# Zero rows for the unused token slots: scattered by number instead of filled over all slots

## The chip, the cores and the metric

The kernel runs on one core of a Trainium2 chip. The metric is the device time of one execution in microseconds. Before the change it is 575.49 us, the median of 3 runs (574.5 to 575.81).

## What is computed

The input `x` is 4 sequences of 512 tokens with 256 numbers each (2048 tokens). It is normalised, and the result `xn` goes two ways. One is a gated linear attention block with an MLP (`s`); the other a mixture of experts (`g`). The output joins them:

```python
xn = _layernorm(x)
# attention: q, k, v, g and a decay per head, then for each time step
S = S * jnp.exp(gt)[..., None] + kt[..., None] * vt[..., None, :]
ot = jnp.einsum('bhk,bhkd->bhd', qt, S)
# then head norm, silu gate, Wo, rmsnorm, MLP
# experts: 16 of them, the best 4 for each token, weights normalised over the 4
act = jax.nn.silu(g) * u
out = jnp.einsum('bske,keh->bskh', act, down_proj)
sel = jnp.take_along_axis(out, top_idx[..., None], axis=2)
return jnp.sum(sel * top_w[..., None], axis=2)
# whole: x + s * silu(experts)
```

## The kernel before

All waits between engines are written out by hand as semaphores; each engine runs its own list in order.

**Routing and slots.** Every (token, expert) pair gets a slot. The slots of one expert fill whole tiles of 128, so 80 tiles (10240 slots, `SLOTS`) are set aside for 8192 pairs; 2048 slots stay without a token. A slot is a row of `rows_scratch` in device memory with 274 numbers (`ROW`): the normalised token, its scale, its token number and its expert weights. A row without a token must hold zeros and a token number beyond the real ones, since the expert stage multiplies it and adds the result to the row of that number in `y_scratch`.

**The zero fills.** `zrow` on the chip is such an empty row for each of 128 partitions (written by POOL, L487 and L488). ScalarE (ACT) issues 16 DMAs (`zero`, L636, called at L700) of 640 rows each, two in each step `u` of the first batch's attention, each behind one activation that normalises `xn` (L698). They cover all 10240 rows and count up `zero_fill`. Eight more fills of `y_scratch` (`y_zero`) come later.

**Order in the first batches.** The attention of a batch takes 8 steps `u`. In a step, VectorE (DVE) does `kv` (L951) and two scans `st` (L959); GpSimd (POOL) multiplies them by q (`product`, L529); TensorE sums them up (`read_out`, L1247). The k and decay of a batch lie in PSUM banks, which ACT fills for the next batch in `next_banks` (L677), when the last `kv` and the last scan of the batch are done. DVE computes the routing (L985 to L1037) as a chain of instructions that wait for each other; between them it puts pieces of the recurrence of steps 6 and 7 of batch 0 and 0 and 1 of batch 1. At its end it counts up `route_ready`; `name_tiles` (L1042 to L1047) then says which expert owns a tile.

**The scatters.** POOL writes the rows to their slots with 64 indirect DMAs of 128 rows (`scatter`, L558). From batch 1's step 0 on it issues two in each step, behind the step's `product`. Ahead of the first pair it waits for `route_ready` and `zero_fill`. The loop `turns` runs on when the products are over, so the last 16 scatters follow one another at once. SyncE (SP) waits for all of them before it loads 16 tiles of rows into `X` (L452), and behind those it issues the two loads of the down weights `wd` (L448), of 14 and of 2 experts. TensorE waits for both `wd` loads after the first tile's gate and up products, ahead of its loop over the tiles.

**The expert stage.** For each of 80 tiles TensorE transposes X (L1276), does 6 gate and up products (L315), transposes the hidden rows (L1374) and does 4 down products; ACT and DVE do what lies between, and POOL adds the result to `y_scratch` (L586). At the end DVE, ACT and POOL combine it with `xn` and `x`.

The line that counts for the entry into this stage:

```python
sp.wait_ge(s["tpn_ready"], KC * B)
sp.wait_ge(s["scatter"], 16 * NT * TOP)
for u in range(UN):
    load_rows(0, u)
load_down(0, E - 2)
sp.wait_ge(s["gu_ready"], 2 * NF * B)
load_down(E - 2, E)
...
gate_up(0, 0, e_first)
pe.wait_ge(s["wd_in"], 32)
tiles(0, True, False)
```

Of the kernel before, what the change touches and what calls it, by code (L numbers as in the profile page):

```python
# [5 lines left out]
F32 = mybir.dt.float32  # L6
# [3 lines left out]
U32 = mybir.dt.uint32  # L10
ALU = mybir.AluOpType
# [3 lines left out]
P = 128  # L15
# [24 lines left out]
def build_block(nc, x, Wq, Wk, Wkg1, Wkg2, bkg2, Wv, Wg, bg, Wo, ln1_w, ln2_w, W1, W3, W2,  # L40
# [3 lines left out]
    T = B * L  # L44
# [14 lines left out]
    SLOT_TILES = -(-(T * TOP // P + E - 1) // 4) * 4  # L59
    SLOTS = SLOT_TILES * P  # L60
    ROW = D + 2 + E
    SCALE_C, TOKEN_C, WEIGHT_C = D, D + 1, D + 2
# [23 lines left out]
    with ExitStack() as ctx:  # L86
# [3 lines left out]
        def sb(name, shape, dt, scope=ctx):  # L90
            return scope.enter_context(nc.sbuf_tensor(name, shape, dt))


        xn = sb("xn", [P, NT, D], F32)
        ident = sb("ident", [P, P], F32)
        ident16 = sb("ident16", [P, P], F16)
# [9 lines left out]
        restart = sb("restart", [P, NT, E], F32)  # L106
        one_e = sb("one_e", [P, E], F32)
        steps128 = sb("steps128", [P, E, NT], F32)
        tile_no = sb("tile_no", [1, SLOT_TILES], F32)
# [29 lines left out]

        zrow_f = sb("zrow", [P, 2 * P + 32], F32, att)  # L140
        zrow = zrow_f[:, 0:ROW]
        sb("fill1", [P, KC * 2 * I - 2 * P - 32], F32, att)

# [18 lines left out]
        def rsb(name, shape=(P, NT, E), dt=F32):  # L162
            return sb(name, list(shape), dt, rt)
# [20 lines left out]
        prod = rsb("prod")  # L184
        slot_f = rsb("slot_f", (P, TOP, NT))
        rt.close()
        pre.close()
# [57 lines left out]
            an_ready anhi_ready anlo_ready xn_ready wk1_t wk1_copied wz_ready rw_t wprep_act wprep_dve w13_in  # L245
            wo_in w2_in zero_fill tp_ready proj_ready evac_act evac_dve z_ready zs_ready
            a_ready dve_chain pool_chain act_chain exp_ready m16_ready cum_ready route_ready ex_in
            scatter zero_row bz_neg wv_mean wv_ready dve_max vt_ready vt_out0 vt_out1 prep_done vr_in0 vr_in1
# [70 lines left out]

        U = HD // 2  # L320
        TOK = lambda b: bass.ds(b * L, L)
        TILES = lambda b, i=0, n=TPB: bass.ds(b * TPB + i, n)
# [53 lines left out]
        def _(sp):  # L376
# [58 lines left out]
            sp.wait_ge(s["gla_used"], U * B + 2)  # L435
            sp.wait_ge(s["zero_fill"], 16 * NT)
            sp.wait_ge(s["y_zero"], 16 * U)
# [16 lines left out]
            sp.wait_ge(s["tpn_ready"], KC * B)  # L454
            sp.wait_ge(s["scatter"], 16 * NT * TOP)
            for u in range(UN):
# [27 lines left out]
        def _(pool):  # L484
# [7 lines left out]
            for m in (ident, ident16):  # L492
# [11 lines left out]
            step(nc.gpsimd.iota(steps128[:, :, :], pattern=[[0, E], [P, NT]], base=0, channel_multiplier=0,  # L504
                                allow_small_or_imprecise_dtypes=True))
            nc.gpsimd.iota(tile_no[:, :], pattern=[[1, SLOT_TILES]], base=0, channel_multiplier=0,
                           allow_small_or_imprecise_dtypes=True).then_inc(s["const_pool"], 1)
# [45 lines left out]

            scatters = iter([(t, j) for t in range(NT) for j in range(TOP)])

            def scatter(n):
                for _, (t, j) in zip(range(n), scatters):
                    nc.gpsimd.indirect_dma_start(  # L558
                        rows_dram, bass.IndirectOffsetOnAxis(ap=slot_u[:, j, t:t + 1], axis=0),
                        rows[:, t, :], None).then_inc(s["scatter"], 16)  # L560

            def step_fn(a, b, c, u):
                if a is not None:
                    if u == 0:
                        pool.wait_ge(s["evac_act"], len(ACT_NTH) * a + ACT_NTH[Q_OUT])
                    product(a, u)
                if b == 0 and u == 0:
                    pool.wait_ge(s["route_ready"], 1)
                    pool.wait_ge(s["zero_fill"], 16 * NT)
                if b is not None:  # L570
                    scatter(2)

            turns(pool, step_fn)
            pool.wait_ge(s["pool_turn"], U * B)
            pool.wait_ge(s["scatter"], 16 * NT * TOP)

# [26 lines left out]
        def _(act):  # L603
# [87 lines left out]
            for u in range(U):  # L691
# [4 lines left out]
                for t in (2 * u, 2 * u + 1):  # L696
                    act.wait_ge(s["an_ready"], t + 1)
                    nc.scalar.activation(xn[:, t, :], xn[:, t, :], ACT.Identity, scale=rsq[:, 0, t:t + 1],  # L698
                                         bias=shift[:, 0, t:t + 1]).then_inc(s["xn_ready"], 1)
                    zero(rows_dram[t * (SLOTS // NT):(t + 1) * (SLOTS // NT)], "zero_fill")  # L700
                if u == 4:
# [144 lines left out]
        def _(dve):  # L846
# [177 lines left out]
            step(nc.vector.tensor_tensor(base[:, :], ntc[:, :], ntl[:, :], ALU.subtract))  # L1024
            step(nc.vector.tensor_scalar(base[:, :], base[:, :], float(P), None, ALU.mult))
            step(nc.vector.tensor_tensor(inc[:, :, :], inc[:, :, :], tot[:, :, :], ALU.subtract))
            step(nc.vector.tensor_tensor(slot[:, :, :], CUM, inc[:, :, :].rearrange("p e t -> p t e"), ALU.add))
# [4 lines left out]
            for j in range(TOP):  # L1032
# [3 lines left out]
                step(nc.vector.tensor_reduce(slot_f[:, j, :], prod[:, :, :], AX.X, ALU.add))  # L1036
            nc.vector.tensor_copy(slot_u[:, :, :], slot_f[:, :, :]).then_inc(s["route_ready"], 1)  # L1037

            def name_tiles():
# [392 lines left out]
```

## Time and profile before

| | us |
|---|---|
| median of 3 runs | 575.49 (574.5 to 575.81) |
| the profiled execution | 574.92 |
| its span, first to last instruction | 572.9 |
| PE busy | 429.3 (75%) |
| DVE busy | 345.0 (60%) |
| POOL busy | 304.7 (53%) |
| ACT busy | 230.9 (40%) |
| DMA, mean share of the 16 engines | q1 (SP) 31.6%, q0 (POOL) 20.0%, q10 (ACT) 8.5% |

PE is TensorE's matmuls. The share of busy time is a mean over stages with different limits: up to about 345 us the engines take turns in the attention, from there on the expert stage runs. L followed by a number is a line of the kernel. In a timeline a row says when an instruction started, how long it took, on which engine and line, and in brackets how long the engine had been idle before it and for what; a "q" behind an engine's name is its queue of orders, DMA issues among them. "issue" stands for time in which the engine waited for nothing that the profile shows. Time from issue to landing is that of a DMA.

### The profile page before, as it was taken

The page shows a single profiled execution, that of the slowest core. Times are in us where ns is not written, and L with a number is a line of the kernel's source. Part 1 is how long each engine was busy: PE and PEld are TensorE (multiplying, and loading weights), DVE is VectorE, ACT ScalarE, POOL GpSimd, SP SyncE. Part 2 cuts the span into 40 slices and gives each one's busy share as a digit, 9 for nine tenths or more (in the row PEclk, how much of TensorE's full clock was granted, in tenths as well). Part 3 has the DMA queues.
Part 4 walks back from the last instruction along what each step waited for, and adds up shares of the span by engine and source line. Part 5 has one row for each costly group of instructions (what it writes and reads, how often), then busy time and mean ns, then how long its engine had stood idle before and what let it go on. Part 6 is the DMA issues. An engine that isn't in the chain of part 4 may idle for free.

```text
span 572.9 us, 8861 instructions
## 1 busy us (share of the span) xinstructions
PE 429.3 (75%) x2170; PEld 254.9 (44%) x2171; DVE 345.0 (60%) x613; ACT 230.9 (40%) x521; POOL 304.7 (53%) x230
## 2 busy tenths in 40 slices
PE   2479970313568798699889989999999999999400
PEld 1134320101223354255465557767767767677200
DVE  4665867999989979985755633333333333333065
ACT  0526642300133132122554525556655656566221
POOL 4052695146768468576720006656566656666535
PEclk9989996655759899899999999999999999999855
DMA  8334998745535234232988845666666666664493
GB/s 265 110 111 160 304 330 279 270 150 171 186 123 185 89 126 151 106 114 65 357 288 238 176 149 85 112 101 114 103 112 112 112 102 110 111 85 57 55 318 121
DMA packets 78616, 90.42 MB, mean 158 GB/s; under 512 B 7704, under 2 KB 66808, under 8 KB 78584
## 3 DMA queue, kind: packets, MB, share of 16 engines
q1 hardware_dynamic: 47584, 54.82, 31.6%
q0 software_dynamic: 14592, 19.47, 20.0%
q10 hardware_dynamic: 16408, 15.73, 8.5%
q8 instruction: 16, 0.26, 0.2%
q14 instruction: 16, 0.13, 0.1%
HBM read 50.66 MB, written 39.34 MB: 157 GB/s over the span
## 4 chain that ended last, share of the span: by engine, by line
PE 54%; DVE 19%; issue 9%; DMA 8%; POOL 4%; ACT 2%; ACTq 2%; SPq 0%; POOLq 0%; DVEq 0%
PE mm_ps L315 33%; PE sum_ps L315 12%; DVE st L959 4%; PE turn_ps L1276 3%; DVE kv L951 3%; PE mm_ps L1374 3%; POOL qs L529 2%; DMA rows_scratch<-zrow 2%; DMA eb<-n_L_ffn_expert_bias_dram 2%; PE sum_ps L1247 2%; DVE w_gu L1181 2%; DMA vrep<-v_scratch 1%; DMA y_scratch<-y,X 1%; ACTq L636 1%; DVE ghead L1111 1%
## 5 line engine op out<-in xcount | busy, mean ns | idle before, releaser
L586 POOL DMA_INDIRECT y_scratch<-y,X x80 | 124.3, 1554 | 126.7 <-ACT y L815 96.6
L315 PE MATMUL mm_ps<-w_gu,xT 128*128 x480 | 103.9, 352 | 1.6 <-DVEq L1159 1.5
L529 POOL TENSOR_TENSOR qs<-st,q_sb 128x1024 f32<-128x1024 f32 x32 | 75.4, 2356 | 49.0 <-DVE st L959 24.3
L1071 DVE TENSOR_TENSOR xT<-turn_ps,xT 128x256 f16<-128x256 f32 x80 | 33.9, 425 | 88.0 <-ACT xT L726 88.0
L315 PE MATMUL sum_ps<-wd,hT 112*128 x320 | 82.4, 380 | 0.0
L558 POOL DMA_INDIRECT rows_scratch<-rows,slot_u x64 | 64.0, 1001 | 27.2 <-issue 15.1
L959 DVE TENSOR_TENSOR_SCAN st<-sum_ps,kv 128x512 f32<-128x512 f32 x64 | 75.1, 1210 | 1.0
L315 PE MATMUL mm_ps<-an2T,w 128*128 128x512 f16 x264 | 65.1, 403 | 13.6 <-DVE h_mlp L1080 11.1
L1247 PE MATMUL sum_ps<-qs,sumk 128*32 128x512 f32 x128 | 38.2, 710 | 38.5 <-POOL qs L529 37.2
L315 PEld LDWEIGHTS mm_ps<-w_gu,xT 128*128 128x128 f16 x480 | 46.6, 97 | 33.0 <-issue 2.7
L1164 DVE SCALAR_TENSOR_TENSOR h<-mm_ps,X,sl 128x224 f32<-128x224 f32 x80 | 36.1, 451 | 40.9 <-ACT sl L799 40.9
L315 PEld LDWEIGHTS sum_ps<-wd,hT 112*128 112x128 f32 x320 | 54.3, 190 | 4.7 <-issue 0.2
L815 ACT ACTIVATE y<-sum_ps,X 128x256 f32<-128x256 f32 x80 | 38.0, 474 | 44.3 <-PE sum_ps L315 44.3
L799 ACT ACTIVATE sl<-mm_ps,X 128x224 f32<-128x224 f32 x80 | 35.8, 447 | 43.4 <-PE mm_ps L315 43.4
L315 PE MATMUL mm_ps<-anT,w_a 128*128 128x512 f16 x168 | 43.0, 414 | 11.2 <-DVE anT L912 9.2
L315 PEld LDWEIGHTS mm_ps<-an2T,w 128*128 128x128 f16 x264 | 26.3, 103 | 54.1 <-issue 16.6
L315 PE MATMUL mm_ps<-w,h_mlp 128*128 128x256 f32 x192 | 47.8, 394 | 1.0 <-DVE h_mlp L1080 1.0
L951 DVE TENSOR_TENSOR kv<-vrep,mm_ps 128x1024 f32<-128x1024 f32 x32 | 38.8, 1212 | 5.6 <-ACT mm_ps L677 4.1
L315 PEld LDWEIGHTS mm_ps<-w,h_mlp 128*128 128x128 f32 x192 | 33.9, 189 | 14.5 <-issue 10.0
L732 ACT ACTIVATE sg<-mm_ps 128x512 f32<-128x512 f32 (+1 forms) x24 | 14.3, 597 | 46.8 <-PE mm_ps L315 46.8
L1276 PE MATMUL turn_ps<-ident,X 128*128 128x128 f32 x160 | 30.7, 274 | 2.5 <-issue 2.5
L315 PEld LDWEIGHTS mm_ps<-anT,w_a 128*128 128x128 f16 x168 | 16.9, 105 | 34.9 <-issue 17.8
(165 smaller groups left out, 533.4 us busy)
## 6 DMA issues: line engine op xcount, KB each, us to landing
vrep<-v_scratch SPq DMA_DIRECT2D x64, 256.0 KB
rows_scratch<-zrow ACTq DMA_DIRECT2D x16, 685.0 KB, 11.7
X<-rows_scratch SPq DMA_DIRECT2D x80, 137.0 KB, 2.6
w_gu<-y_scratch SPq DMA_DIRECT2D x16, 256.0 KB, 6.1
y_scratch<-zrow ACTq DMA_DIRECT2D x6, 640.0 KB, 5.9
w_gu<-in_L_ffn_gate_proj_dram SPq DMA_DIRECT2D x16, 224.0 KB, 6.8
w_gu<-in_L_ffn_up_proj_dram SPq DMA_DIRECT2D x16, 224.0 KB, 7.1
wd<-in_L_ffn_down_proj_dram SPq DMA_DIRECT2D x1, 3136.0 KB, 17.4
```

What stands on the lines that cost most here:

```text
L315: last = nc.tensor.matmul(out_ap, lhsT, rhs, start=(n == 0), stop=(n == len(pairs) - 1))
L529: nc.gpsimd.tensor_tensor(qs[:, u % 2, :, :], st[:, u % 2, :, :], pair_bc(q_sb[:, TOK(a)]), ALU.mult).then_inc(s["qs_ready"], 1)
L558: nc.gpsimd.indirect_dma_start(rows_dram, bass.IndirectOffsetOnAxis(ap=slot_u[:, j, t:t + 1], axis=0), rows[:, t, :], None).then_inc(s["sc ...
L586: nc.gpsimd.indirect_dma_start(y_dram[u % 2], bass.IndirectOffsetOnAxis(ap=X[:, u, TOKEN_C:TOKEN_C + 1].bitcast(U32), axis=0), y[:, u, :], ...
L799: nc.scalar.activation(sl[:, u % 2, :], M[u % 2][:, 0:I], ACT.Silu, scale=X[:, u, SCALE_C:SCALE_C + 1])\
L815: nc.scalar.activation(y[:, u, :], sum_ps[:, u % 2, 0:D], ACT.Copy, scale=X[:, u, bass.ds(e + WEIGHT_C, 1)])\
L951: nc.vector.tensor_tensor(kv[:, r, :, :], vrep[:, r, :, :], pair_bc(K_BANK), ALU.mult).then_inc(s["kv_ready"], 1)
L959: nc.vector.tensor_tensor_scan(st[:, r, j, :], A_BANK, kv[:, r, j, :], 0.0, ALU.mult, ALU.add).then_inc(s["st_ready"], 1)
L1071: nc.vector.tensor_tensor(xT[:, u % 2, 1, :, :].rearrange("p c n -> p (c n)"), PS[u % 2][:, 0:KC * P], xT[:, u % 2, 0, :, :].rearrange("p ...
L1164: nc.vector.scalar_tensor_tensor(out=h[:, u % 2, :], in0=M[u % 2][:, I:2 * I], scalar=X[:, u, SCALE_C:SCALE_C + 1], in1=sl[:, u % 2, :], o ...
L1247: last = nc.tensor.matmul(O0[rows_at:rows_at + QUARTER, :], sumk[:, off:off + QUARTER], qs[:, u % 2, j, :], start=(dd % PER == 0), stop=(d ...
L1276: last = nc.tensor.transpose(PS[u % 2][:, n * P:(n + 1) * P], X[:, u, n * P:(n + 1) * P], ident[:, :])
```

## The change

ACT's 16 zero fills and the semaphore `zero_fill` go. The numbers of the 2048 slots without a token are computed by DVE: four instructions on 128x16 join the routing chain, and five (three of them on 128x256) follow behind `route_ready` and count up `pads_ready`. POOL writes the empty rows to them with 16 indirect DMAs of 128 rows. The row scatters start at step 2 of batch 1 rather than at step 0, and the four that this displaces are done in the last round of `turns`, in which there are no products; the 16 scatters of empty rows stand there too, four in each of the first four steps. SP and POOL wait for 80 scatters in place of 64.

```diff
+    PADS = SLOTS - T * TOP
+    NPAD = PADS // P
...
+        zrow = sb("zrow", [P, ROW], F32)
...
+        pad_no = sb("pad_no", [P, NPAD], F32)
+        pad_u = sb("pad_u", [P, NPAD], U32)
...
+        held, pads_to, past, pad_f = mx, need, eqc[:, 0:NPAD, :], sm[:, 0:NPAD]
...
+        SCATTER_FROM = 2
...
-            sp.wait_ge(s["zero_fill"], 16 * NT)
...
-            sp.wait_ge(s["scatter"], 16 * NT * TOP)
+            sp.wait_ge(s["scatter"], 16 * (NT * TOP + NPAD))
...
+            step(nc.gpsimd.iota(pad_no[:, :], pattern=[[P, NPAD]], base=0, channel_multiplier=1,
+                                allow_small_or_imprecise_dtypes=True))
...
+            def scatter_pads(n):
+                for _, i in zip(range(n), pads):
+                    nc.gpsimd.indirect_dma_start(
+                        rows_dram, bass.IndirectOffsetOnAxis(ap=pad_u[:, i:i + 1], axis=0),
+                        zrow[:, :], None).then_inc(s["scatter"], 16)
...
-                if b == 0 and u == 0:
+                if b == 0 and u == SCATTER_FROM:
                     pool.wait_ge(s["route_ready"], 1)
-                    pool.wait_ge(s["zero_fill"], 16 * NT)
-                if b is not None:
+                if b == 1 and u == 0:
+                    pool.wait_ge(s["pads_ready"], 1)
+                if b is not None and (b > 0 or u >= SCATTER_FROM):
                     scatter(2)
+                if b == B - 1 and u < U // 2:
+                    scatter(2)
+                    scatter_pads(-(-NPAD // (U // 2)))
...
-                    zero(rows_dram[t * (SLOTS // NT):(t + 1) * (SLOTS // NT)], "zero_fill")
...
+            step(nc.vector.tensor_tensor_scan(held[:, :], one_e[:, :], inc[:, :, NT - 1:NT].rearrange("p e a -> p (e a)"), 0.0,
+                                              ALU.mult, ALU.add))
+            step(nc.vector.tensor_tensor(pads_to[:, :], base[:, :], held[:, :], ALU.subtract))
+            step(nc.vector.tensor_copy(held[:, :], inc[:, :, NT - 1:NT].rearrange("p e a -> p (e a)")))
+            step(nc.vector.tensor_tensor(pads_to[:, :], pads_to[:, :], held[:, :], ALU.add))
...
             nc.vector.tensor_copy(slot_u[:, :, :], slot_f[:, :, :]).then_inc(s["route_ready"], 1)
+
+            of_e = lambda ap: ap.rearrange("p (a e) -> p a e", a=1).to_broadcast((P, NPAD, E))
+            step(nc.vector.tensor_tensor(past, of_e(pads_to[:, :]),
+                                         pad_no[:, :].rearrange("p (i a) -> p i a", a=1).to_broadcast((P, NPAD, E)), ALU.is_le))
+            step(nc.vector.tensor_tensor(past, past, of_e(held[:, :]), ALU.mult))
+            step(nc.vector.tensor_reduce(pad_f, past, AX.X, ALU.add))
+            step(nc.vector.tensor_tensor(pad_f, pad_f, pad_no[:, :], ALU.add))
+            nc.vector.tensor_copy(pad_u[:, :], pad_f).then_inc(s["pads_ready"], 1)
```

## Rows read from the trace of the kernel before

**Rows 1.** Busy time by stretch (us, PE, PEld, DVE, ACT, POOL, clock, DMA share, GB/s)

```profile
345.00:525.00 180.00, 178.20 (x1017) 127.18 (x1016) 63.26 (x145) 107.05 (x290) 112.81 (x73) 1.00 0.64 103
315.00:320.00 5.00, 5.00 (x25) 2.29 (x24) 3.38 (x4) 2.83 (x5) 0.00 (x0) 1.00 1.13 256
189.00:193.00 4.00, 3.89 (x11) 1.48 (x12) 3.96 (x6) 0.60 (x1) 0.00 (x0) 0.58 0.09 35
```

**Rows 2.** The chain of waits, 80 to 135 us (start us, us, what)

```profile
97.99 12.98 DMA rows_scratch<-zrow
...
111.01 10.68 issue
```

**Rows 3.** Timeline of ACT near 100 us (start, us, engine, line, what [idle before])

```profile
100.43 0.60 ACT L677 ACTIVATE mm_ps<-k_sb 128x512 f32<-128x512 f32 x1 [1.86 <-issue]
```

**Rows 4.** Timeline of DVE, 90 to 127 us

```profile
93.31 2.27 DVE L1000 TENSOR_TENSOR_SCAN eqc<-restart,eq 128x256 f32<-128x256 f32 x1
...
101.16 1.22 DVE L951 TENSOR_TENSOR kv<-vrep,mm_ps 128x1024 f32<-128x1024 f32 x1 [4.15 <-ACT mm_ps L677]
102.30 0.42 DVE L1003 TENSOR_TENSOR eq<-eq,eqc 128x256 f32<-128x256 f32 x1
...
111.42 0.69 DVE L1017 TENSOR_TENSOR_SCAN inc<-restart,tot 128x256 f32<-128x256 f32 x1
...
113.28 0.17 DVE L1024 TENSOR_TENSOR base<-ntc,ntl 128x16 f32<-128x16 f32 x1
...
125.03 1.86 DVE L1047 TENSOR_SCALAR tile_expert<-own 1x80 uint32<-1x80 f32 x1
126.81 1.20 DVE L951 TENSOR_TENSOR kv<-vrep,mm_ps 128x1024 f32<-128x1024 f32 x1
```

**Rows 5.** Timeline of POOL, 92 to 127 us

```profile
92.19 2.85 POOL L539 TENSOR_TENSOR w<-w_raw,w 128x1408 f16<-128x1408 f32 x1
96.86 2.35 POOL L529 TENSOR_TENSOR qs<-st,q_sb 128x1024 f32<-128x1024 f32 x1 [1.83 <-DVE st L959]
108.29 2.36 POOL L529 TENSOR_TENSOR qs<-st,q_sb 128x1024 f32<-128x1024 f32 x1 [9.08 <-PE sum_ps L1247]
...
124.47 2.35 POOL L529 TENSOR_TENSOR qs<-st,q_sb 128x1024 f32<-128x1024 f32 x1
```

**Rows 6.** Timeline of POOL, 263 to 290 us

```profile
263.99 2.35 POOL L529 TENSOR_TENSOR qs<-st,q_sb 128x1024 f32<-128x1024 f32 x1 [3.54 <-DVE st L959]
...
279.18 0.96 POOL L558 DMA_INDIRECT rows_scratch<-rows,slot_u  x1 [0.30 <-issue]
...
288.97 1.23 POOL L558 DMA_INDIRECT rows_scratch<-rows,slot_u  x1 [0.30 <-issue]
```

**Rows 7.** All instructions on `rows_scratch`, their DMAs

```profile
DMA to landing us min/median/max: 2.0/2.8/13.3
```

**Rows 8.** Timeline of the SP queue, 300 to 322 us

```profile
300.45 7.46 SPq L452 DMA_DIRECT2D X<-rows_scratch  x16
307.95 13.82 SPq L448 DMA_DIRECT2D wd<-in_L_ffn_down_proj_dram  x2
```

**Rows 9.** DMA issues between 300 and 340 us (x, KB each, us to landing)

```profile
wd<-in_L_ffn_down_proj_dram SPq DMA_DIRECT2D x1, 3136.0 KB, 17.4
X<-rows_scratch SPq DMA_DIRECT2D x16, 137.0 KB, 3.3
...
wd<-in_L_ffn_down_proj_dram SPq DMA_DIRECT2D x1, 448.0 KB, 7.4
```

**Rows 10.** Timeline of PE, around 189 us and 336 us

```profile
176.95 2.76 PE L315 MATMUL mm_ps<-an2T,w 128*128 128x512 f16 x12
...
189.11 4.34 PE L315 MATMUL mm_ps<-an2T,w 128*128 128x512 f16 x12 [4.73 <-DVE h_mlp L1080]
...
321.26 0.60 PE L1276 MATMUL turn_ps<-ident,X 128*128 128x128 f32 x4
...
336.36 1.31 PE L315 MATMUL mm_ps<-w_gu,xT 128*128 x6 [1.53 <-DVEq L1159]
```

More of the change, by code:

```diff
@@ L60, in build_block @@
     SLOTS = SLOT_TILES * P
+    PADS = SLOTS - T * TOP
+    NPAD = PADS // P
+    assert PADS % P == 0
     ROW = D + 2 + E
@@ L138, in build_block @@
         qs = sb("qs", [P, 2, 2, L], F32, att)
-        zrow_f = sb("zrow", [P, 2 * P + 32], F32, att)
-        zrow = zrow_f[:, 0:ROW]
-        sb("fill1", [P, KC * 2 * I - 2 * P - 32], F32, att)
+        sb("fill1", [P, KC * 2 * I], F32, att)
         g_sb = sb("g_sb", [P, KC, T], F32, att)
@@ L245, in build_block @@
             an_ready anhi_ready anlo_ready xn_ready wk1_t wk1_copied wz_ready rw_t wprep_act wprep_dve w13_in
-            wo_in w2_in zero_fill tp_ready proj_ready evac_act evac_dve z_ready zs_ready
-            a_ready dve_chain pool_chain act_chain exp_ready m16_ready cum_ready route_ready ex_in
+            wo_in w2_in tp_ready proj_ready evac_act evac_dve z_ready zs_ready
+            a_ready dve_chain pool_chain act_chain exp_ready m16_ready cum_ready route_ready pads_ready ex_in
             scatter zero_row bz_neg wv_mean wv_ready dve_max vt_ready vt_out0 vt_out1 prep_done vr_in0 vr_in1
@@ L554, in _ @@
             scatters = iter([(t, j) for t in range(NT) for j in range(TOP)])
+            pads = iter(range(NPAD))
             def scatter(n):
@@ L566, in step_fn @@
                     product(a, u)
-                if b == 0 and u == 0:
+                if b == 0 and u == SCATTER_FROM:
                     pool.wait_ge(s["route_ready"], 1)
-                    pool.wait_ge(s["zero_fill"], 16 * NT)
-                if b is not None:
+                if b == 1 and u == 0:
+                    pool.wait_ge(s["pads_ready"], 1)
+                if b is not None and (b > 0 or u >= SCATTER_FROM):
                     scatter(2)
+                if b == B - 1 and u < U // 2:
+                    scatter(2)
+                    scatter_pads(-(-NPAD // (U // 2)))
             turns(pool, step_fn)
             pool.wait_ge(s["pool_turn"], U * B)
-            pool.wait_ge(s["scatter"], 16 * NT * TOP)
+            pool.wait_ge(s["scatter"], 16 * (NT * TOP + NPAD))
             pool.sem_inc(s["y_slots"], UN)
```

## The prediction

> **What bounds the kernel now.** I read the busy time by stretch first. From 345 to 525 us TensorE is busy for 178.2 of 180 us at the full granted clock [rows 1]: the expert stage is TensorE's alone, so whatever the change does before it reaches the end undiminished, and nothing after it can absorb a delay. The change touches two earlier places, the routing (80 to 127 us) and the entry into the expert stage (265 to 340 us).
>
> The chain of waits names the last zero fill, 12.98 us from its issue to its landing at 110.97, and then 10.68 us of "issue" [rows 2]. That is not the price of the fill: POOL's wait for it ends at 110.97, but the slot numbers it also waits for exist only at 121.69. What the fills do cost is ScalarE's time. Its queue issues them, and the bank fills of batch 1 (L677) stand behind the last of them; the first starts at 100.43, with "issue" as the reason for the idle time [rows 3]. VectorE waits for that bank: 4.15 us idle before the `kv` product at 101.16 [rows 4], in the middle of its otherwise unbroken routing work. That wait is the gain to be had.
>
> **Part 1: the zero fills go.** With ScalarE free, the K bank is filled as soon as `kv_ready` allows, before 97.0, when VectorE is free (101.16 less 4.15). The A bank needs the last scan of batch 0, done just before POOL's product at 96.86 [rows 5], plus a 0.60 copy [rows 3]: 97.5, wanted at 98.2, when `kv` is done. So the whole 4.15 goes. -4.15.
>
> **What is late next.** POOL's products then meet VectorE elsewhere. The rows show the effect: the 128x256 scan L1000 takes 2.27 us while POOL works from 92.19 to 95.04, the scan of the same shape L1017 takes 0.69 with POOL idle, and L1047, on 80 numbers, takes 1.86 beside the product at 124.47 [rows 4, 5]. The Trainium skill, "SBUF — State Buffer", section "Who interferes with whom", says that a VectorE instruction with two SBUF inputs contends with a GpSimd instruction that reads SBUF, the later one waiting for the whole of the other; the rows just named agree, and without the rule the front part would come out at about -3.1.
> - L1003 moves from 102.30 to 98.15, inside POOL's product of 96.86 to 99.21. It ends some 0.25 after that instead of at 98.57: +0.9.
> - `product(1, 1)` no longer waits behind `route_ready`. Before, it runs at 124.47. Its state and read-outs are ready when `product(1, 0)` ends, so it follows at once: 105.0 to 107.4 for the first (108.29 less 3.25), to 109.75 for the second. L1017 would start at 108.2; by L1000, which ends 0.54 after POOL, it ends at 110.3 and not at 108.9: +1.4.
> - The other side: L1047 no longer has a product beside it. At about 0.25 us for its 80 numbers: -1.6.
>
> **Part 2: the numbers of the pads, on VectorE.** Four instructions on 128x16 stand ahead of `route_ready`; such a one takes 0.17 (L1024) [rows 4], with the gap of a chained step some 0.21: +0.85. After it come three on 128x256 at 0.42 (as L1003) and two small ones, 1.8 us with gaps. POOL scatters nothing yet, so these don't hold it, but `name_tiles` and the next `kv` (126.81) stand behind them on VectorE: +1.8.
> Front sum: -4.15 + 0.9 + 1.4 + 0.85 + 1.8 - 1.6 = **-0.8**. Bounds: -3.1 with no collision; +0.2 if POOL keeps VectorE out over both products; I take the sum that reads each collision from its nearest row. The iota for `pad_no` and the larger constants stand at the start, under the wait for the first loads: 0.
>
> From there to 266 us POOL does two scatters beside each product, as before; only the first four move. The 4 extra row scatters thus fall to the end, where VectorE and TensorE set the pace, and all carry the -0.8.
>
> **Part 3: 20 more scatters behind the last product.** Before, 18 scatters follow the product of 263.99 and the last starts at 288.97. After, 4 more of rows and 16 of pads follow. Each takes 0.96 and 0.30 of idle time, 1.26 [rows 6]; a pad's has the same shape. 20 x 1.26 = 25.2, so the last starts at 288.97 + 25.2 - 0.8 = 313.4, and with the 2.8 us median to landing [rows 7] it is there at 316.2.
>
> Who waits: SyncE's queue has `scatter` ahead of the 16 loads of X, and both `wd` loads stand behind those. Before, SyncE goes on at 300.45, on TensorE's word; the scatters were no matter. It spends 7.46 us on the X loads and issues the large `wd` load at 307.95 [rows 8], which lands 17.4 later; the small one takes 7.4, much of it behind the large one [rows 9]. After: X from 316.2. The first X tile lands by 319.5 with the 3.3 of [rows 9]; TensorE turns it at 321.26 [rows 10] less 0.8: hidden, by 1 us only. The large `wd` is issued at 316.2 + 7.5 = 323.7 and lands at 341.1; the small one directly behind it, by bytes 17.4 x 448/3136 = 2.5, at 343.6.
>
> TensorE waits for both before its tile loop, right after its first six expert products (336.36 + 1.31 = 337.67 [rows 10], less 0.8 = 336.9). Stall: 343.6 - 336.9 = **6.7**. Bounds: 3.4 (the small load rides along, landing 2.0) to 12 (21 us for both, as from 307.95 to the last landing before, and 6.8 us of queueing for the scatters).
>
> **Part 4: the clock after the stall.** After 4.73 us of idle time twelve products take 4.34 instead of 2.76 [rows 10], at a granted clock of 0.58 of full speed in that stretch, the lower level of 1.2 GHz for most of it [rows 1]. A stall of 6.7 should do the same: **+1.6** (bounds 0 and 4).
>
> **Sum.** -0.8 + 6.7 + 1.6 = +7.5. The profiled execution took 574.92 (span 572.9); 582.4 for it, and against the median of 575.49, which is 0.57 above it: **583.0**.
>
> **The rivals.**
> - *The weights are in time (faster).* TensorE waits only if `wd` is in later than 336.9, so 3.67 MB within 13.2 us of 323.7, 278 GB/s. For it: the large load alone ran at 185 GB/s while it shared the engines with the last X loads, and TensorE would need only 6.7 us. Against it: from 315 to 320, with nothing but `wd` moving, the 16 engines were full (share 1.13) at 256 GB/s [rows 1]. Then the front decides: 575.49 - 0.8 to - 3.1, 572.4 to 574.7. Chance 0.17. The Trainium skill, "DMA: Bandwidth & Descriptors", section "Measured (HBM→SBUF, 128 partitions, SWDGE, issued from GpSimd)", has 1 MB at 341 GB/s; an estimate from that page is 11 us for both loads and no stall, but the 17.4 measured here for the same transfer decides.
> - *Between:* the scatters land sooner and the small load costs nothing; a stall near 3.4, little loss of clock, front at -3.1 to -0.8: 576.5 to 580. Chance 0.13.
> - *No gain in front:* the bank comes late for another reason (POOL's last product, a load of `vrep`), and only the added work is left: +3.35 instead of -0.8, with the same stall behind it: 587. Chance 0.12. For it: VectorE never waited on anything else there, so nothing shows what is next. Against: each producer is done by 97.5.
> - *Main case,* 580 to 586.5: 0.58.
>
> **How the numbers follow.** The forecast is the main case's, 583.0. A range of 576.5 to 588 takes in the two slower cases and the between one; what is left out is mostly the rival of in-time weights. This kernel's measurement tells 0.2% (1.15 us) from no change: faster 0.16, same 0.06, slower 0.78.
>
> **What would show it.** Right: no ScalarE DMA issue of `rows_scratch`; the 4.15 us before L951 gone; the L1017 scan near 2 us; 38 scatters behind the last product, ending near 315; SyncE's wait for `scatter` some 16 us longer; the `wd` loads issued near 324; TensorE idle for 6 to 7 us at 337 to 344. Wrong: no gap on TensorE there; POOL done before 305; or the first `kv` of batch 1 still late.

## The result, and the profile after

| | before | after |
|---|---|---|
| median | 575.65 us, 4 runs (574.5 to 575.97) | 586.32 us, 4 runs (584.51 to 587.26) |
| the profiled execution | 574.92 | 587.26 |
| its span | 572.9 | 585.3 |
| DVE busy | 345.0 | 348.7 |
| POOL busy | 304.7 | 321.7 |

The ratio is 1.0185, 95% interval [1.0156, 1.0214]: slower by some 10.7 us. The two profiled executions, which the working compares, differ by 12.34 us.

Lines of the kernel after are numbered anew: `kv` L968, `st` L976, `product` L536, the bank fills L695, row scatters L566, scatters of empty rows L572, the matmul helper L320, the turning of X L1306; on SP the loads of X L457 and of `wd` L453.

The queues first: ACT's (q10) carried 15.73 MB and 8.5% of the DMA engines before; after, the same view of the page has

```profile
q1 hardware_dynamic: 47584, 54.82, 32.8%
q0 software_dynamic: 15360, 21.72, 20.7%
q10 hardware_dynamic: 5912, 4.51, 2.5%
```

So the fills are gone and 11.2 MB with them; POOL's queue (q0) carries 2.25 MB more. ACT's timeline in the stretch of [rows 3] has no issue of `rows_scratch` any more, and both banks come early:

```profile
92.28 0.60 ACT L695 ACTIVATE mm_ps<-k_sb 128x512 f32<-128x512 f32 x1 [1.79 <-DVE kv L968]
97.74 0.60 ACT L695 ACTIVATE sum_ps<-a_sb 128x512 f32<-128x512 f32 x1 [4.86 <-DVE st L976]
```

DVE's timeline answers to [rows 4]:

```profile
86.57 1.57 DVE L1012 TENSOR_TENSOR gt<-lg,m 128x256 f32<-128x256 f32 x1
...
97.95 1.21 DVE L968 TENSOR_TENSOR kv<-vrep,mm_ps 128x1024 f32<-128x1024 f32 x1
99.08 1.44 DVE L1020 TENSOR_TENSOR eq<-eq,eqc 128x256 f32<-128x256 f32 x1
...
109.22 2.27 DVE L1034 TENSOR_TENSOR_SCAN inc<-restart,tot 128x256 f32<-128x256 f32 x1
...
113.08 0.19 DVE L1043 TENSOR_TENSOR_SCAN mx<-one_e,inc 128x16 f32<-128x16 f32 x1
...
121.68 0.20 DVE L1059 CAST slot_u<-slot_f 128x64 uint32<-128x64 f32 x1
121.79 0.42 DVE L1062 TENSOR_TENSOR eqc<-need,pad_no 128x256 f32<-128x256 f32 x1
...
126.79 0.19 DVE L1077 TENSOR_SCALAR tile_expert<-own 1x80 uint32<-1x80 f32 x1
126.91 1.20 DVE L968 TENSOR_TENSOR kv<-vrep,mm_ps 128x1024 f32<-128x1024 f32 x1
```

The `kv` at 97.95 has no idle time in front of it where 4.15 us were. But L1020 takes 1.44 instead of 0.42 and the scan L1034 2.27 instead of 0.69, both beside a product of POOL; the naming is fast (0.19 for 1.86). The `kv` behind it starts at 126.91, against 126.81 before: the front has gained nothing.

The price stands at the entry of the expert stage. POOL's timeline first (compare [rows 6]), the last product and then 38 scatters, of which three stand here:

```profile
264.75 2.35 POOL L536 TENSOR_TENSOR qs<-st,q_sb 128x1024 f32<-128x1024 f32 x1 [3.55 <-DVE st L976]
...
274.89 0.96 POOL L572 DMA_INDIRECT rows_scratch<-zrow,pad_u  x1 [0.30 <-issue]
...
286.32 1.86 POOL L572 DMA_INDIRECT rows_scratch<-zrow,pad_u  x1 [0.30 <-issue]
...
316.22 0.96 POOL L566 DMA_INDIRECT rows_scratch<-rows,slot_u  x1 [0.30 <-issue]
```

SP waited 25.2 us for them ahead of the X loads (before, 1.8, and then 5.0 for TensorE). Its queue's timeline, then the DMA issues between 310 and 360 us (x, KB each, us to landing), against [rows 8] and [rows 9]:

```profile
318.89 7.46 SPq L457 DMA_DIRECT2D X<-rows_scratch  x16
326.40 10.49 SPq L453 DMA_DIRECT2D wd<-in_L_ffn_down_proj_dram  x2
336.94 2.28 SPq L467 DMA_DIRECT2D xback<-in_L_attn_x_dram  x1
```

```profile
wd<-in_L_ffn_down_proj_dram SPq DMA_DIRECT2D x1, 3136.0 KB, 18.5
...
xback<-in_L_attn_x_dram SPq DMA_DIRECT2D x1, 2048.0 KB, 17.1
wd<-in_L_ffn_down_proj_dram SPq DMA_DIRECT2D x1, 448.0 KB, 21.7
```

The first `wd` load is issued 18.45 us later than before, and the second lands at 348.6 (issued at 326.9, 21.7 on). TensorE stands still until then, as PE's timeline (against [rows 10]) and the busy time by stretch (columns as in [rows 1]) show:

```profile
337.20 1.31 PE L320 MATMUL mm_ps<-w_gu,xT 128*128 x6 [1.53 <-DVEq L1189]
349.42 0.66 PE L1306 MATMUL turn_ps<-ident,X 128*128 128x128 f32 x2 [10.91 <-DMA wd<-in_L_ffn_down_proj_dram]
349.87 2.45 PE L320 MATMUL mm_ps<-w_gu,xT 128*128 x6
...
354.55 1.03 PE L320 MATMUL sum_ps<-wd,hT 112*128 x4
```

```profile
340.00:345.00 5.00, 0.00 (x0) 0.00 (x0) 0.00 (x0) 0.00 (x0) 0.00 (x0) 0.50 1.13 222
345.00:350.00 5.00, 0.58 (x3) 0.52 (x4) 0.00 (x0) 0.00 (x0) 0.00 (x0) 0.50 1.10 301
350.00:355.00 5.00, 5.00 (x22) 2.97 (x21) 1.30 (x3) 2.04 (x6) 0.00 (x0) 0.66 0.35 109
```

Between 340 and 345 us every compute engine is at zero and the DMA engines are full: only loads are under way, those of the down weights and, behind them, the 2 MB of `xback`. From the turn at 349.42 to the first down product, 5.13 us pass where it took 4.28 before. The same rows of the kernel before:

```profile
337.55 0.41 PE L1276 MATMUL turn_ps<-ident,X 128*128 128x128 f32 x2
...
340.14 0.41 PE L1276 MATMUL turn_ps<-ident,X 128*128 128x128 f32 x2 [0.74 <-issue]
...
341.83 1.03 PE L315 MATMUL sum_ps<-wd,hT 112*128 x4
```

The granted clock was 0.50 from 340 to 350 us (the lower level, 1.2 GHz), and the first six products behind the wait take 2.45 us for 1.31. The restart costs 0.85 us net, because the 0.74 us for which TensorE stood idle at 340.14 in the kernel before are gone.

So the 12.4 us are: entry of the stage (PE's products at 337.20 against 336.36) +0.84, wait +10.91, clock +0.85, sum 12.6. Behind the last matmul 0.5 us come back (36.4 us to the end for 36.9).

### The profile page after: what moved, and what is told of

Read it like the earlier page. It is cut to its first block and busy times, and to the rows that moved or that the text cites. A ratio compares the mean times of both kernels' runs of the same rounds, so it can differ in the third digit from the quotient of the medians.

```text
span 585.3 us, 8870 instructions
## 1 busy us (share of the span) xinstructions
PE 429.6 (73%) x2170; PEld 255.5 (44%) x2171; DVE 348.7 (60%) x622; ACT 231.0 (39%) x521; POOL 321.7 (55%) x247
## 5 line engine op out<-in xcount | busy, mean ns | idle before, releaser
L536 POOL TENSOR_TENSOR qs<-st,q_sb 128x1024 f32<-128x1024 f32 x32 | 75.5, 2362 | 64.6 <-DVE st L976 55.8
L320 PE MATMUL mm_ps<-w_gu,xT 128*128 x480 | 105.2, 356 | 1.6 <-DVEq L1189 1.5
L320 PE MATMUL sum_ps<-wd,hT 112*128 x320 | 82.3, 380 | 0.0
L976 DVE TENSOR_TENSOR_SCAN st<-sum_ps,kv 128x512 f32<-128x512 f32 x64 | 75.0, 1209 | 1.0
L320 PE MATMUL mm_ps<-an2T,w 128*128 128x512 f16 x264 | 64.0, 398 | 15.2 <-DVE h_mlp L1110 12.7
L566 POOL DMA_INDIRECT rows_scratch<-rows,slot_u x64 | 62.8, 981 | 16.3 <-issue 15.4
L320 PEld LDWEIGHTS mm_ps<-w_gu,xT 128*128 128x128 f16 x480 | 47.0, 98 | 33.7 <-issue 3.8
L320 PEld LDWEIGHTS sum_ps<-wd,hT 112*128 112x128 f32 x320 | 54.3, 190 | 4.6 <-issue 0.2
L320 PE MATMUL mm_ps<-anT,w_a 128*128 128x512 f16 x168 | 43.1, 415 | 11.7 <-DVE anT L929 9.6
L320 PEld LDWEIGHTS mm_ps<-an2T,w 128*128 128x128 f16 x264 | 26.0, 102 | 54.8 <-issue 15.0
L320 PE MATMUL mm_ps<-w,h_mlp 128*128 128x256 f32 x192 | 47.8, 394 | 1.0 <-DVE h_mlp L1110 1.0
L1306 PE MATMUL turn_ps<-ident,X 128*128 128x128 f32 x160 | 31.2, 277 | 12.9 <-DMA wd<-in_L_ffn_down_proj_dram 10.9
L320 PEld LDWEIGHTS mm_ps<-w,h_mlp 128*128 128x128 f32 x192 | 33.9, 189 | 14.5 <-issue 10.0
L968 DVE TENSOR_TENSOR kv<-vrep,mm_ps 128x1024 f32<-128x1024 f32 x32 | 38.7, 1210 | 0.7 <-DVE vt L944 0.4
L743 ACT ACTIVATE xT<-turn_ps 128x256 f16<-128x256 f32 x80 | 30.0, 376 | 12.4 <-PE turn_ps L1306 12.3
## 6 DMA issues: line engine op xcount, KB each, us to landing
wd<-in_L_ffn_down_proj_dram SPq DMA_DIRECT2D x1, 3136.0 KB, 18.5
```

The costliest lines, as they stand in the source:

```text
L320: last = nc.tensor.matmul(out_ap, lhsT, rhs, start=(n == 0), stop=(n == len(pairs) - 1))
L536: nc.gpsimd.tensor_tensor(qs[:, u % 2, :, :], st[:, u % 2, :, :], pair_bc(q_sb[:, TOK(a)]), ALU.mult).then_inc(s["qs_ready"], 1)
L566: nc.gpsimd.indirect_dma_start(rows_dram, bass.IndirectOffsetOnAxis(ap=slot_u[:, j, t:t + 1], axis=0), rows[:, t, :], None).then_inc(s["sc ...
L968: nc.vector.tensor_tensor(kv[:, r, :, :], vrep[:, r, :, :], pair_bc(K_BANK), ALU.mult).then_inc(s["kv_ready"], 1)
L976: nc.vector.tensor_tensor_scan(st[:, r, j, :], A_BANK, kv[:, r, j, :], 0.0, ALU.mult, ALU.add).then_inc(s["st_ready"], 1)
L1306: last = nc.tensor.transpose(PS[u % 2][:, n * P:(n + 1) * P], X[:, u, n * P:(n + 1) * P], ident[:, :])
```

## The experiments

Theory: the loss is the wait of TensorE for `wd`, and it comes from the number of scatters behind the last product, by way of SP's queue; the front is a gain and a cost that cancel. Rivals: the added VectorE work or the delayed first scatters cost the time; the load is slow by itself; the fills' removal is worth nothing.

Each is compared with runs of the kernel before on the same chip, whose median there was 573.6 us for `from0`, `x2_first`, `pads_mid` and `late_fills`, 574.09 for `displaced`, `pads_half`, `xback_late` and `combo`, and 584.91, on a third chip, for `before_again`, `late_again` and `numbers`. Four positions are read from each trace: the start of the routing on DVE (`lg`), the `kv` behind the naming, the first products of the expert stage (the "entry"), and the end.

**1. Four scatters fewer behind the last product.** `from0`:

```diff
-        SCATTER_FROM = 2
+        SCATTER_FROM = 0
```

> The changed kernel with the row scatters started at step 0 of batch 1 again, so that four fewer stand behind the last product (34 in place of 38). My theory: the time behind the last product goes straight into TensorE's wait for the down weights; 4 x 1.26 = 5.1 us less there, a wait of 5.8 us in place of 10.9, and 586.3 - 5.1 = 581 us. In front the product of step 1 stands behind the routing again: the scan of the counts back to 0.7 us, the naming of the tiles slower by 1.6, so nothing at the first kv after it. Rival (the weights are late because of the DMA traffic, not of the order on SyncE's queue): the wait stays at 10 to 11 us, 586 us.

Measured: 578.87 us, ratio 1.009 [1.0061, 1.0118]. SP goes on at 313.58. PE's timeline and the landings:

```profile
334.44 1.30 PE L320 MATMUL mm_ps<-w_gu,xT 128*128 x6 [1.53 <-DVEq L1189]
340.61 0.66 PE L1306 MATMUL turn_ps<-ident,X 128*128 128x128 f32 x2 [4.87 <-DMA wd<-in_L_ffn_down_proj_dram]
```

```profile
wd<-in_L_ffn_down_proj_dram SPq DMA_DIRECT2D x1, 3136.0 KB, 16.5
...
wd<-in_L_ffn_down_proj_dram SPq DMA_DIRECT2D x1, 448.0 KB, 18.2
```

The wait fell from 10.91 to 4.87, by 6.0 us, near the 5.1 expected, but not as expected. Counted from POOL's last product (261.99 here, 264.75 in the kernel after), SP goes on only 2.5 us sooner (51.6 for 54.1): two more scatters were slow in this profile (1.88 and 1.82 us), and the last one landed later. The other 3.5 us are the loads': both are in 18.7 us after the first was issued, for 22.2. So the wait falls with the number of scatters at the end, but one pair of profiles doesn't give a price for one.

**2. The order on SP.** `x2_first` (all scatters stay where the change put them):

```diff
-            for u in range(UN):
+            for u in range(2):
                 load_rows(0, u)
             load_down(0, E - 2)
             sp.wait_ge(s["gu_ready"], 2 * NF * B)
             load_down(E - 2, E)
+            for u in range(2, UN):
+                load_rows(0, u)
```

> The changed kernel with SyncE's order altered behind its wait for the scatters: two tiles of X, then both loads of the down weights, then the other 14 tiles of X. Theory: the weights start 14 x 0.467 = 6.5 us sooner and have 1.9 MB fewer ahead of them; TensorE's wait falls from 10.9 to 4 us or so, 579 to 580 us. Rival (something else holds TensorE there, such as the loads of x for the end): no change, 586 us.

Measured: 573.63 us, ratio 0.9998 [0.9969, 1.0028], better than the 579 to 580 expected. SP's queue, the landings and PE:

```profile
317.44 0.82 SPq L457 DMA_DIRECT2D X<-rows_scratch  x2
318.30 7.54 SPq L453 DMA_DIRECT2D wd<-in_L_ffn_down_proj_dram  x2
```

```profile
wd<-in_L_ffn_down_proj_dram SPq DMA_DIRECT2D x1, 3136.0 KB, 15.7
...
wd<-in_L_ffn_down_proj_dram SPq DMA_DIRECT2D x1, 448.0 KB, 15.1
```

```profile
335.75 1.31 PE L320 MATMUL mm_ps<-w_gu,xT 128*128 x6 [1.53 <-DVEq L1191]
336.95 0.41 PE L1308 MATMUL turn_ps<-ident,X 128*128 128x128 f32 x2
```

The wait is gone, and with it the whole loss, although 38 scatters still stand at the end. Here the first load is issued 8.1 us sooner than in the kernel after. The small one is issued at 320.84 and lands at 335.9, so both are in 17.6 us after the first was issued instead of 22.2, with 14 X loads behind them instead of ahead (issued from 325.89 on) and `xback` (2 MB, issued at 334.99) only at their end. TensorE wants them when its six products are done, at 337.06: 1.1 us to spare. So the loss needs SP's order, in which 14 tiles of X that nobody wants yet stand before weights that TensorE waits for. The rival that added work makes the loss falls: all of it is still in this kernel (what it costs alone is experiment 8).

**3. and 4. The scatters of empty rows in the middle.** `pads_mid` puts one behind each product's pair in batches 2 and 3, `pads_half` puts eight there and leaves eight at the end (23 and 30 scatters behind the last product; the forecast below counts 22). The edit of `pads_mid`:

```diff
+                if b in (1, 2):
+                    scatter_pads(1)
                 if b == B - 1 and u < U // 2:
                     scatter(2)
-                    scatter_pads(-(-NPAD // (U // 2)))
```

> The changed kernel with the 16 scatters of empty rows spread over batches 2 and 3 (one in each step) instead of behind the last product. Theory: 22 scatters behind the last product end near 295 us, before SyncE's other wait ends at 301; no wait for the down weights; what is left is the front of the change, +0.8 us by the two traces, so 576.5 us, and up to 578 if POOL's added 1.26 us a step reach the chain of waits. Rival (POOL has no room in these batches and becomes the bound): over 580 us. Rival (the change's cost lies elsewhere than behind the last product): near 586 us.

> The changed kernel with 8 of the 16 scatters of empty rows in batch 2 and 8 behind the last product: 30 there in place of 38. Theory (a threshold, no price per scatter): SyncE goes on 10.1 us sooner, the weights land near 336 and TensorE wants them at 338: no wait or one under 1 us, ratio to the kernel before 1.000 to 1.002. Rival (each scatter there costs its share, 12 us over 16 scatters): half of the loss, ratio 1.009.

Measured: 574.61, ratio 1.0002 [0.9976, 1.0029], where 576.5 was expected, and 574.73, ratio 1.0001 [0.9974, 1.0028]. No wait for `wd` in either; in `pads_half` both loads are in at 335.4, and TensorE is through its six products at 339.0. With `from0` and the kernel after, this makes a curve:

| scatters at the end | SP goes on | `wd` issued | wait of PE | ratio |
|---|---|---|---|---|
| 23 (`pads_mid`) | 298.75 | 306.25 | 0 | 1.0002 |
| 30 (`pads_half`) | 308.50 | 316.64 | 0 | 1.0001 |
| 34 (`from0`) | 313.58 | 321.09 | 4.87 | 1.009 |
| 38 (after) | 318.89 | 326.40 | 10.91 | 1.0185 |

The price is a threshold, not a price per scatter: from 23 to 30 nothing, then 4.87 us of waiting for the next four and 6.04 for the last four. Part of these steps is how fast the loads landed, as experiment 1 shows.

**5. Only the scatters displaced.** `displaced` is the kernel before, with its fills, whose scatters start at step 2 and whose last four stand in the last round:

```diff
-                if b == 0 and u == 0:
+                if b == 0 and u == 2:
                     pool.wait_ge(s["route_ready"], 1)
                     pool.wait_ge(s["zero_fill"], 16 * NT)
-                if b is not None:
+                if b is not None and (b > 0 or u >= 2):
                     scatter(2)
+                if b == B - 1 and u < 2:
+                    scatter(2)
```

> The kernel before with only the order of the row scatters changed as in the changed kernel: none at steps 0 and 1 of batch 1, the four in the last round; the zero fills stay. 22 scatters stand behind the last product and end near 295 us, the last landing near 301, about when SyncE's other wait ends. Theory: the down weights come 1 us later at most, with 8 us to spare, so nothing there; in front the product of step 1 moves ahead of the routing and collides with the scan of the counts (+1.6) but no longer with the naming of the tiles (-1.6): 0 within 0.3, ratio 1.000. Rival (the displaced scatters cost something by themselves): 1.003 or more.

Measured: 575.49 us, ratio 1.0022 [0.9997, 1.0046], no wait for `wd`. The interval holds the 1.000 expected and the rival's 1.003, so the time decides neither; from `lg`, the entry comes at 254.68 against 254.81. Two rows of DVE:

```profile
99.76 1.22 DVE L953 TENSOR_TENSOR kv<-vrep,mm_ps 128x1024 f32<-128x1024 f32 x1 [4.01 <-ACT mm_ps L679]
...
110.02 2.27 DVE L1019 TENSOR_TENSOR_SCAN inc<-restart,tot 128x256 f32<-128x256 f32 x1
```

With the fills kept the wait for the bank stays (4.01 for 4.15): it is the fills' doing. And the slow scan belongs to the displaced scatters: `product(1, 1)`, no longer held behind `route_ready`, runs beside it. In `from0`, where the scatters start at step 0 and the product waits again (POOL's next product starts at 120.85), the scan is fast.

**6. Only two fills out of the way.** `late_fills` is the kernel before; its last two zero fills are issued behind the bank fills instead of ahead of them. Nothing is left out:

```diff
-                    zero(rows_dram[t * (SLOTS // NT):(t + 1) * (SLOTS // NT)], "zero_fill")
+                    if u < U - 1:
+                        zero(rows_dram[t * (SLOTS // NT):(t + 1) * (SLOTS // NT)], "zero_fill")
...
             next_banks(0)
+            for t in (NT - 2, NT - 1):
+                zero(rows_dram[t * (SLOTS // NT):(t + 1) * (SLOTS // NT)], "zero_fill")
```

> The kernel before with one edit: the two zero fills of ScalarE's last step are issued behind the bank fills of batch 1 instead of ahead of them. Theory: the 4.15 us in which VectorE waits for the bank go, less 0.9 for a collision with POOL's product; 575.65 - 3.3 = 572.4 us. Rival (the wait only moves, for example to the fills that now land late for POOL): 575 to 576 us.

Measured: 569.94 us, ratio 0.9929 [0.9903, 0.9956]: **faster than both kernels**. ACT's timeline:

```profile
92.12 0.58 ACT L677 ACTIVATE mm_ps<-k_sb 128x512 f32<-128x512 f32 x1
94.81 0.60 ACT L677 ACTIVATE sum_ps<-a_sb 128x512 f32<-128x512 f32 x1 [2.11 <-DVE st L962]
94.82 5.02 ACTq L636 DMA_DIRECT2D rows_scratch<-zrow  x2
```

Counted from `lg`, the `kv` behind the naming comes at 42.06 instead of 45.26. But at the entry only 0.84 of these 3.2 us are left. Where they go the two traces show: twice TensorE pauses for VectorE and then does twelve products at a lower granted clock. In the kernel before the first dozen is the 4.34 us of [rows 10]; the second dozen there, and both here:

```profile
239.71 4.45 PE L315 MATMUL mm_ps<-an2T,w 128*128 128x512 f16 x12 [4.83 <-DVE h_mlp L1080]
```

```profile
184.31 5.30 PE L315 MATMUL mm_ps<-an2T,w 128*128 128x512 f16 x12 [5.29 <-DVE h_mlp L1083]
...
236.11 5.30 PE L315 MATMUL mm_ps<-an2T,w 128*128 128x512 f16 x12 [4.84 <-DVE h_mlp L1083]
```

The granted clock is 0.50 and 0.51 over the two dozens here, 0.62 and 0.61 in the kernel before. Counted from `lg`, the `kv` during the first dozen is 2.86 us sooner than in the kernel before and the next one 1.67; at the second dozen 1.66 becomes 0.81. The clock took 1.8 of the 3.2 us. What is left, with 0.73 less from the entry to the end, is 1.6 us, less than the 3.7 by which the medians differ. So the kernel was run once more beside a profile of the kernel before, on the third chip.

**7. The same again.** `before_again` and `late_again` are the kernel before and `late_fills`, unchanged.

> The kernel before, unchanged, once more with a profile, as the partner of late_again on the same chip. Theory and rival alike: from the start of the routing (lg) to VectorE's kv behind the naming 45.3 us, to the entry of the expert stage 254.8, from there to the end of the span 236.5, each within some 0.3. What it tells is how far these marks move between two profiled executions of one program: if by 1 us or more, then the shift of 0.8 us that late_fills kept at the entry of the expert stage is no finding.

> The same kernel as late_fills, timed again. Theory A: its gain is real and is more than its one profile explained, ratio near 0.993. Theory B: only what its profile showed at the entry of the expert stage (0.84 us) and behind it (0.73) is real, 1.57 of 574, ratio near 0.997. Theory C: nothing is left of it, ratio 0.999 to 1.001. In the profile, for all three: kv behind the naming 3.2 us earlier after the start of the routing, and 0.5 to 1.2 us of that left at the entry of the expert stage.

Measured for `late_again`: 582.07 us against 584.91, ratio 0.9944 [0.9921, 0.9967]. The gain is real on both chips. In the profiles, from `lg`: `kv` at 42.08 against 45.42, 3.34 sooner; POOL's last product 0.91 sooner (0.84 in the first pair), most of the rest lost to the dozens, which again take 5.30 and 5.22 us for 4.19 and 4.45; entry at 265.24 in both, nothing left; end 1.36 sooner from there, all of it behind the last matmul. The profile of `before_again` agrees with the first one to 0.3 us up to POOL's last product, then its entry is 10.4 us later. There PE and ACT pause with the DMA engines full, and the clock falls; PE's timeline and the stretch 285 to 290 us:

```profile
278.81 2.54 PE L315 MATMUL mm_ps<-an2T,w 128*128 128x512 f16 x6 [2.26 <-issue]
288.49 6.13 PE L315 MATMUL mm_ps<-an2T,w 128*128 128x512 f16 x18 [7.14 <-issue]
```

```profile
285.00:290.00 5.00, 1.51 (x4) 0.59 (x5) 0.00 (x0) 2.17 (x3) 2.03 (x3) 0.50 1.09 370
```

What they wait for the trace doesn't say. That the DMA engines are full isn't enough: in the first profile they were as full (share 1.09, 380 GB/s, from 280 to 285 us) without such a pause. Marks at the entry thus move by more than the 0.84 us that I had read as the gain. That the median gains 2.8 to 3.7 us, where the profiles account for 1.4 to 1.6 behind `lg`, stays open.

**8. Only the numbering.** `numbers` is the kernel before with the `iota` and the nine VectorE instructions of the change added; nothing reads their result, and fills and scatters are as before.

```diff
+            step(nc.vector.tensor_tensor_scan(held[:, :], one_e[:, :], ...
...
             nc.vector.tensor_copy(slot_u[:, :, :], slot_f[:, :, :]).then_inc(s["route_ready"], 1)
+            step(nc.vector.tensor_tensor(past, of_e(pads_to[:, :]), ...
...
+            nc.vector.tensor_copy(pad_u[:, :], pad_f).then_inc(s["pads_ready"], 1)
```

> Before, with fills and scatters as they were, plus the nine VectorE instructions of the numbering (and the iota), whose result nothing reads. Theory: they cost 0.85 us behind the scan and 1.85 us behind the slots, so kv behind the naming is 2.65 to 2.7 us later after the start of the routing; of that the middle of the kernel takes up the greater part, as it took up the 3.2 us of late_fills, so 0.3 to 1.2 us are left at the entry of the expert stage and the ratio is 1.001 to 1.002. Rival: the shift goes through whole, 2.65 us at the entry of the expert stage, ratio 1.0046.

Measured: 587.25 us, ratio 1.0036 [1.0014, 1.0058], 2.3 us. Two rows of DVE:

```profile
99.53 1.22 DVE L958 TENSOR_TENSOR kv<-vrep,mm_ps 128x1024 f32<-128x1024 f32 x1 [3.26 <-ACT mm_ps L684]
...
125.78 0.72 DVE L1067 TENSOR_SCALAR tile_expert<-own 1x80 uint32<-1x80 f32 x1
```

The instructions last what was forecast, but `kv` is only 0.64 us later after `lg` than in `before_again` (46.06, 45.42), not 2.65: the wait for the bank took up 1.05, the last naming instruction slid off POOL's product (1.14 less). Yet the entry is 3.65 later. Of that, 2.63 are there at POOL's last product already (184.96 us after `lg` for 182.33), ahead of the pause: the dozens of products take 5.30 and 5.29 us for 4.19 and 4.45, so TensorE's clock added 1.95. The last 1.0 comes in the pause. Both of my readings missed the way, though the rival's 1.0046 lies in the interval, by luck.

**9. `xback` out of the way.** `xback_late` is the kernel after, with the 2 MB load of `x` behind the loop over all X tiles:

```diff
-            sp.dma_start(xback_f[:, :, :], xr).then_inc(s["xr_in"], 16)
             with sp.Fori(1, GROUPS) as g:
...
                     load_rows(g, u)
+            sp.dma_start(xback_f[:, :, :], xr).then_inc(s["xr_in"], 16)
```

> The changed kernel with the load of x for the end (2 MB) issued behind all tiles of X instead of ahead of the second group. In the changed kernel it is issued at 336.9, while the down weights are under way, and both of those land 22 us after the first issue, where I had reckoned 19.9. Theory: this load shares the engines with them; without it they land after 19.5 to 20.5 us and the wait falls from 10.9 to about 9: ratio 1.015. Rival (the weights take as long on their own): 10.9 us and 1.018 as before.

Measured: 585.66 us, ratio 1.0208 [1.0161, 1.0254]. Both `wd` loads are in 19.3 us after the first was issued (22.2 in the kernel after), 2.9 sooner. The theory holds in this, but not all of the 2.9 need be `xback`'s: in `from0` the loads took 18.7 with it. The wait is 9.37 and not 8.0, since SP went on 1.4 later after the last product. From the last matmul to the first load of the combining stage 10.4 us pass where the kernel after takes 7.7, and the ratio is no better than the 1.0185 of the kernel after; the 1.015 expected lies outside the interval.

**10. The best of the parts.** `combo` scatters from step 0, puts the empty rows in the middle and moves their numbering into step 6 of batch 1:

```diff
-        SCATTER_FROM = 2
+        SCATTER_FROM = 0
...
+                if b in (1, 2):
+                    scatter_pads(1)
...
+                        if b == 0:
+                            number_pads()
```

> Three edits of the changed kernel at once: the empty rows scattered one a step in batches 2 and 3, the row scatters from step 0 of batch 1 as in the kernel before, and the five instructions that number the pads moved from behind the routing to step 6 of batch 1, where VectorE waits a microsecond for ScalarE anyway. Theory: no wait for the weights; front 0.5 us better than before by the order of the products, 1.8 us better by the five instructions, of which 0.8 come back at step 6, and the collision of the scan gone: 2 us less than before, ratio 0.9965. Rival (the front has no influence on the end): 1.000.

Measured: 574.03 us, ratio 1.0005 [0.9979, 1.0031]. The 0.9965 expected was missed. `kv` is 1.95 us sooner after `lg`, the entry 1.1 later. The moved numbering met a product: L1062 takes 2.23 instead of 0.42. `late_fills` remains the fastest version.

## Why the prediction was right and where it was off

The forecast was 583.0 with a range of 576.5 to 588; the median is 586.32, just inside the main case's 580 to 586.5. The mechanism is the one foretold, and `x2_first` and `pads_mid` show it: take away either SP's order or the pile of scatters, and the whole loss goes. The size is less good: the terms measured sum to 12.6 us in the profiled execution where 7.5 were forecast. That the medians differ by only 10.7 helped. The terms:

| term | forecast | measured |
|---|---|---|
| wait for the bank (Part 1) | -4.15 | -4.15 |
| L1020 beside the product | +0.9 | +1.0 |
| L1034 beside the product | +1.4 | +1.6 |
| four small instructions | +0.85 | +0.85 |
| five behind the slots | +1.8 | +1.5 |
| naming's last instruction | -1.6 | -1.7 |
| entry of the expert stage, all in all | -0.8 | +0.84 |
| wait for `wd` (Part 3) | +6.7 | +10.9 |
| clock (Part 4) | +1.6 | +0.85 |

- **Part 1 and its collisions** hold row by row. The Trainium skill, "SBUF — State Buffer", section "Who interferes with whom", has a VectorE instruction with two SBUF inputs and a reading GpSimd instruction exclude each other; the two collisions forecast from rows came as it says. (L1047, which the prediction names beside them, has one input, so that rule doesn't cover it; its 1.86 and 0.19 us are what the rows show.) One was not foreseen: L1012 takes 1.57 for 0.41, beside POOL's L544, against 0.9 saved on `lg` (0.44 for 1.33); the start of POOL's own work had moved a little. Counted from `lg`, `kv` is 0.51 us sooner, not 0.8; `lg` itself was 0.61 later, and in the thirteen profiles of this study it lies anywhere from 78.5 to 82.2.
- **The step that failed in the front** is "all carry the -0.8": that a shift at 127 us goes through undiminished to 337. The 0.51 was +0.23 at the entry, and the 3.2 to 3.3 of `late_fills` were 0.8 and 0 there. VectorE is not the only engine that sets the pace between: TensorE's products behind its two pauses run at a clock that differs from run to run. In the kernel after the two dozens take 4.49 and 4.73 us for 4.34 and 4.45, 0.4 of the 0.74 us between -0.51 and +0.23; in `late_fills` they take 1.8 of 3.2, in `numbers` they add 1.95 to 0.64.
- **The mis-sized term is the stall,** by 4.2 us. The `wd` load was issued 2.7 later than forecast (326.40 for 323.7): 1.6 because the last product was late instead of early, 1.3 because 20 scatters took 26.5 and not 25.2, a few of them 1.2 to 1.9 us long; the landing gave 0.1 back (2.7, where 2.8 was taken). That 2.8 was a misreading that did no harm: [rows 7] takes in the loads of X, and the 64 scatters alone have 2.4/3.8/6.8. Both loads took 22.2 us instead of 19.9, and from 336.94 on `xback` shares the engines with them: SP's very next order, which I had not counted. TensorE went on 0.8 behind the landing, where I had put nothing. Against it: TensorE was ready 1.6 later. 2.7 + 2.3 + 0.8 - 1.6 = 4.2. The bound of 12 held; the value taken inside it was the small load's share by bytes, 2.5 us, and its landing came 3.7 behind the large one's.
- **The clock term** was taken from twelve products in a row. Here the restart is a mixed chain with other engines in between: TensorE's longer products fill 0.74 us in which it stood idle before, so the lower clock (0.50, then 0.66 from 350 to 355 us) cost 0.85 net.
- **The rival of weights in time** needed 278 GB/s. It did not come in the kernel after, where 3.67 MB took 22.2 us, 165 GB/s. Even with fewest X loads ahead (`x2_first`) both took 17.6, 208 GB/s. The Trainium skill's "DMA: Bandwidth & Descriptors", section "Measured (HBM→SBUF, 128 partitions, SWDGE, issued from GpSimd)", from which the estimate of 11 us came, is not borne out for this transfer by any run here: the least was 17.6.
- **No gain in front** (rival): refuted at 97.95, where `kv` has no wait; its 587 came nearer to the result than the 583.0 all the same, by luck: its stall was the same 6.7, and the time came from the longer stall.
- **SyncE's wait,** a sign of being right, was put at "some 16 us longer" and came out 23.4 longer (25.2 for 1.8). The 16 is how much later SP was to go on; before, its last wait was for TensorE, 5.0 us behind the one for the scatters, and that was left out. The scatters in the kernel before had landed at 295.36, not at 300.45.

## What to carry to other kernels

When work is appended to one engine's list, follow what waits for its end through every queue behind it, and count the orders that come after the critical one too: the loss here was a threshold (30 scatters free, 38 cost 10.9 us of waiting), and reordering one other queue removed it without touching the added work. Where a stall sits behind DMA issues on the engine that has to copy, moving two of the issues can be enough; here that beat every version that removed all sixteen and added work for it. An advance measured at one place is no advance at the end until a second place confirms it.

## What the runs showed of the hardware

- **A VectorE instruction begun during POOL's DMA_INDIRECT lasted until the product behind it was over.** In batch 1 of the kernel before, DVE's L1111, a `tensor_scalar` on 128x64, starts at 135.02 while POOL is still in a DMA_INDIRECT (134.41 to 135.37), and the product of 135.39 to 137.74 follows; DVE's row and the same one in `late_fills`:

```profile
135.02 2.79 DVE L1111 TENSOR_SCALAR ghead<-ghead 128x64 f32<-128x64 f32 x1
```

```profile
129.88 2.79 DVE L1114 TENSOR_SCALAR ghead<-ghead 128x64 f32<-128x64 f32 x1
```

  It ends just after the product, though it began before it. In later batches a `tensor_tensor` of that size takes 2.91 and 3.05 in the same way, and some 0.23 when alone. The Trainium skill, "SBUF — State Buffer", section "Who interferes with whom", lets `tensor_scalar` enter a mode that holds the shared ports, and says that issue order decides who blocks; that the later product blocks an instruction already begun is seen here only beside a DMA_INDIRECT.
- **The same load took 15.7, 16.5, 17.4 and 18.5 us** (3136 KB of `wd`; `x2_first`, `from0`, before, after), and both loads together 17.6, 18.7 and 22.2 us (`x2_first`, `from0`, after). What else was on the engines differed each time; `xback_late` (19.3) tests one part of it.
- **TensorE's clock behind a pause can swallow a shift, or add to it.** Twelve products of 128x512 take 2.76 us at full clock; behind pauses of 4.7 to 6.3 us they took 4.19 to 5.30, at a granted clock of 0.62 (4.34) to 0.50 (5.30). Moving the work ahead of the pause 2.9 us sooner or 0.5 us later made them longer in both cases.
- **An order for a DMA can be dear on ACT's queue:** two zero fills took 5.02 us to issue in `late_fills` and one 4.97 in `displaced`. One at 57.17 in the kernel before took 0.38, with the DMA engines as full (share 0.99 from 56 to 60 us), so a full set of engines alone doesn't make it dear.
- **One chip was slower at one place.** The kernel before took 574 us on two chips and 584.91 on the third; in the one profile of it there, nearly all of the difference is the pause at 277 to 288 us shown in experiment 7, and `late_again` and `numbers` have it too.
